# Routing of a mixture of experts rebuilt: top two with Max8 and an index search, running sums on TensorE, one-hots by two engines

## The chip, the cores and the metric

One core of a Trainium2 chip runs the whole program. Its five engines run side by side and meet at semaphores: TensorE (PE, matmul; its weight loads are listed as PEld), VectorE (DVE), ScalarE (ACT), GpSimd (POOL) and SyncE (SP), which here only issues transfers. The metric is the device time of one execution in microseconds, and of several executions their median.

## The reference

A decoder layer over 8 x 256 tokens of width 256: linear attention, a gated cross attention (mLSTM), and a mixture of 8 experts. The change touches only the routing in front of the experts:

```
normed = _layernorm(hidden_states, rn_g, rn_b)
logits = (jnp.einsum('bld,ed->ble', normed, router_w) + router_b).astype(jnp.float32)
top_w, top_idx = jax.lax.top_k(logits, K)                      # K = 2 of E = 8
top_w = jax.nn.softmax(top_w, axis=-1).astype(hidden_states.dtype)
onehot = jax.nn.one_hot(top_idx, E, dtype=top_w.dtype)
combine = jnp.einsum('blke,blk->ble', onehot, top_w)
for e in range(E):
    h = _layernorm(hidden_states, ln_g[e], ln_b[e])
    h = jax.nn.gelu(jnp.einsum('bld,di->bli', h, w1[e]) + b1[e], approximate=False)
    h = jnp.einsum('bli,id->bld', h, w2[e]) + b2[e]
    out = out + combine[..., e:e + 1] * h
```

## The kernel before

The 2048 tokens lie as T = 16 tiles of P = 128, token p of tile t in partition p. After the attentions, `mlstm_vector` normalizes the rows of batch b (two tiles) with `hidden_rows(b)`; ScalarE stores them to `hidden_rows` in memory with `store_rows(b)`, TensorE turns them and computes 8 logits per token in `logits(b)`, and `add_bias(b)` on VectorE moves the logits from PSUM to `LG` (T x E per partition). `logits(b)` waits for `add_bias(b - 2)`, since two PSUM banks serve in turn.

The experts work on slots, not on tokens. Every token has two pairs (token, expert), 4096 in all; the slots of an expert are filled in the order of tokens and padded to whole tiles of 128, which makes at most NT = 39 slot tiles. The routing must say for each slot tile which tokens stand in it (`tok_f`), with which weights (`wgt`), and whose expert it is (`tile_e`):

- `experts_vector` finds the greatest logit, its index, masks it out and does the same again (L1774 to L1783, each instruction over all 16 tiles and linked to the one ahead by a semaphore: `link`). `picked` is the sum of the two one-hot planes.
- TensorE counts along the partitions with two matmuls of `picked`: by a triangle (L1676, rank inside a tile) and by ones (L1677, count of each tile).
- VectorE scans these counts over the tiles, rounds the experts' totals up to whole tiles by counting thresholds, and adds up each pair's slot (L1794 to L1814). Three casts split the slot into slot tile and position in it (L1817 to L1820).
- For each of the 32 blocks of 128 pairs VectorE makes a 128-wide one-hot of the position (`posh`, L1825, eight blocks to an instruction) and three planes of 39 (L1830 to L1834: is it this slot tile, times token number, times weight). `posh` lies in `QT` where `hidden_rows` was staged, so the first waits for all stores (`z_st`).
- TensorE multiplies them, 32 accumulated matmuls of 3 x 39 columns (L1685): the result has, at partition p and column n, what slot p of slot tile n holds. Between the counts and these stand nine matmuls whose result nobody reads (`keep_going(9)`, L1673), and behind them six more.
- VectorE repairs the padding slots (L1849, L1850), casts the first token numbers (`tokg`) and signals `tok_r`. GpSimd then fetches the rows of slot tiles 0 and 1 from `hidden_rows` by an indirect transfer (L1640).

The tile loop follows: for each of 39 slot tiles TensorE turns the fetched rows (L1694), multiplies by the expert's `w1` (L1705), ScalarE applies Gelu (L1756), TensorE multiplies by `w2` (L1713), VectorE adds `b2` and scales (L1897, L1900), and GpSimd adds the rows to the output in memory (L1660). The output has been filled with X by SyncE before (L1627), as soon as all stores of `hidden_rows` have landed. The order on every engine is the order in which the code is written; there is no scheduler.

Of the kernel before, what the change touches and what calls it, by code (L numbers as in the profile page):

```python
# [29 lines left out]
C_TOK, C_CNT, C_TILE, C_RESET, C_PAR, C_CENT, C_PAD = 660, 692, 708, 748, 876, 878, 1006  # L30
C_POS, C_SLOT, C_W = 1007, 1135, 1174
# [34 lines left out]
def constants():  # L66
# [47 lines left out]
def build(nc, x_d, ctx_d, ctxr_d, idx_d, cst_d, wqT_d, wkT_d, wvT_d, woT_d, wk_d, gw_d, sw_d, wg_d, gb_d,  # L114
          rpe_d, lnw_d, lnb_d, rng_d, rnb_d, rw_d, rb_d, lg_d, lb_d, w1_d, b1_d, w2_d, b2_d, out_d):
    ctx = ExitStack()
    with ctx:
# [40 lines left out]
        first_slot = cst[:, C_SLOT:C_SLOT + NT]  # L158
# [886 lines left out]
        def parts_at(q):  # L1045
# [50 lines left out]
            sem("hid_r"), sem("hT_full"), sem("hT_cp"), sem("lg_full"), sem("lg_cp"), sem("z_st"))  # L1096
# [234 lines left out]
        def mlstm_scalar(act, at=None):  # L1331
# [103 lines left out]
            act.dma_start(z_dram[B * S:B * S + P], hid[0][:, 0]).then_inc(z_st, 16)  # L1435

        def mlstm_vector(dve):
# [122 lines left out]
            for b in range(4, B):  # L1560
                add_bias(b)
# [3 lines left out]
        def experts():  # L1565
            cl = Carve(PET[:, :, :].rearrange("p a b -> p (a b)"), kept)
            posh = QT[:, :, :, :].rearrange("p j b s -> p (j b s)").rearrange("p (k n) -> p k n", n=P)
            open_, base = cw(NT, E), cw(E)
            ntile, tile_end, tile_f, slot_f = cw(E), cw(E), cw(NT), cw(2 * T)
            b1c = [cw(I // P) for _ in range(2)]  # L1570
            fill_f, tok_f, wgt = cw(NT), cw(NT), cw(NT)
            LG2, EQ = cl(T, E), cl(T, E)
            OH = [cl(T, E) for _ in range(2)]
            picked, upto, slot_of = cl(E, T), cl(E, T), cl(E, T)
            over = LG2.rearrange("p t e -> p (t e)").rearrange("p (e t) -> p e t", e=E)
            M1, M2, IX, PR = cl(T), cl(T), cl(T), cl(T)
            pair_w, pos, first_of = cl(2 * T), cl(2 * T), cl(2 * T)
# [5 lines left out]
            f_ov, f_so, f_hit = sem("f_ov"), sem("f_so"), sem("f_hit")  # L1583
# [17 lines left out]
            NPOS = 8  # L1601
# [23 lines left out]
            def experts_sync(sp):  # L1625
                sp.wait_ge(z_st, 16 * (B + 1))
# [11 lines left out]
            def experts_gpsimd(pool):  # L1638
# [5 lines left out]
                pool.wait_ge(z_st, 16 * (B + 1))  # L1644
# [25 lines left out]
            def experts_tensor(pe):  # L1670
# [3 lines left out]

                pe.wait_ge(f_pk, 1)
                pe.matmul(bank(0, T * E), tri, picked.rearrange("p e t -> p (e t)"), start=True, stop=True)  # L1676
                pe.matmul(bank(1, T * E), ones, picked.rearrange("p e t -> p (e t)"), start=True, stop=True).then_inc(f_ps, 1)  # L1677

                keep_going(9)
                for k in range(2 * T):  # L1680
                    if k % T == 0:
                        pe.wait_ge(wts_r, k // T + 1)
                    if k % NPOS == 0:
                        pe.wait_ge(pos_r, k // NPOS + 1)
# [79 lines left out]
            def experts_vector(dve):  # L1764
# [4 lines left out]
                def wide(a):  # L1769
                    return a.unsqueeze(2).to_broadcast([P, T, E])  # L1770
# [373 lines left out]
```

## Time and profile before

| | us |
|---|---|
| median of three timed runs | 844.79 |
| lowest and highest of them | 840.76, 845.15 |
| the profiled execution, whole | 838.66 |
| its span | 836.9 |
| TensorE matmul busy in the span | 751.9 (90%) |
| VectorE busy | 403.1 (48%) |
| ScalarE busy | 353.4 (42%) |
| GpSimd busy | 429.7 (51%) |
| start of the first matmul of the tile loop | 544.22 |

The span is what the profile covers, and the whole time is that of the same execution with what lies around it. Positions below are microseconds from the span's start. A matmul of 32-bit numbers has two rows in the trace, so 32 of them are "x64". The granted clock of TensorE (PEclk) is a share of full speed.

### The profile page before, as it was taken

What the parts mean: (1) busy time and instruction counts of PE and PEld (TensorE: products, weight loads), DVE (VectorE), ACT (ScalarE), POOL (GpSimd) and SP (SyncE); (2) the same over time, 40 slices, a digit from 0 to 9 for tenths busy, and PEclk for the clock granted to TensorE, in tenths of its full rate; (3) what the DMA queues carried; (4) which work ended last, traced back from release to release, by engine and by line L of the source; (5) the groups of instructions that cost most, each with busy time, mean ns of one, the idle gap of its engine ahead of it and who ended that gap; (6) DMA issues with size and microseconds to landing.
All of it is one profiled execution on the core that took longest, in us unless ns stands there. A gap on an engine that the chain in (4) does not pass through costs nothing.

```text
span 836.9 us, 17067 instructions
## 1 busy us (share of the span) xinstructions
PE 751.9 (90%) x5866; PEld 662.0 (79%) x5867; DVE 403.1 (48%) x966; ACT 353.4 (42%) x916; POOL 429.7 (51%) x504
## 2 busy tenths in 40 slices
PE   7888888878988888898798887999999999999996
PEld 5566666657888878897787775689999999999995
DVE  2456666555554433332569897723333333333331
ACT  1333333324555433332667754144444444444441
POOL 6566666656666666666445541124444444444442
PEclk8999999989999999999889999999999999999999
DMA  9233333343233336356267699322221222122221
GB/s 293 78 102 103 109 113 111 111 121 93 84 92 89 89 89 189 89 108 194 83 185 202 201 282 354 120 77 38 38 38 32 37 38 38 31 38 38 38 36 22
DMA packets 75812, 88.29 MB, mean 106 GB/s; under 512 B 11952, under 2 KB 66032, under 8 KB 75632
## 3 DMA queue, kind: packets, MB, share of 16 engines
q0 software_dynamic: 19824, 43.93, 21.1%
q1 hardware_dynamic: 52256, 40.12, 16.5%
q10 hardware_dynamic: 3680, 3.54, 1.2%
q8 instruction: 34, 0.56, 0.3%
q14 instruction: 18, 0.15, 0.1%
HBM read 75.83 MB, written 11.73 MB: 105 GB/s over the span
## 4 chain that ended last, share of the span: by engine, by line
PE 40%; issue 27%; POOL 14%; DVE 9%; ACT 5%; another core or an unknown queue 3%; DMA 1%; POOLq 1%; DVEq 0%; ACTq 0%
PE ps L1964 15%; POOL out L1660 7%; PE ps L1030 7%; POOL G L1640 5%; PE ps L484 3%; PE ps L525 2%; PE ps L551 2%; DVE U L809 1%; ACT G L1353 1%; DMA out<-G,slots 1%; PE ps L1227 1%; PE ps L1673 1%; PE ps L592 1%; PE ps L477 1%
## 5 line engine op out<-in xcount | busy, mean ns | idle before, releaser
L331 POOL DMA_INDIRECT G<-in_rpe,hopi x193 | 186.6, 967 | 108.2 <-issue 42.1
L1756 ACT ACTIVATE G<-ps,U 128x128 f32<-128x128 f32 x312 | 84.9, 382 | 160.5 <-PE ps L1705 160.5
L1705 PEld LDWEIGHTS ps<-G,QT 128*128 128x128 f32 x1248 | 145.2, 192 | 1.9
L1705 PE MATMUL ps<-G,QT 128*128 128x128 f32 x1248 | 145.5, 275 | 0.0
L1713 PE MATMUL ps<-G 128*128 x624 | 141.2, 379 | 1.3 <-DVE G L1900 1.3
L1713 PEld LDWEIGHTS ps<-G 128*128 128x128 f32 x624 | 115.5, 190 | 15.8 <-issue 1.7
L1964 PE MATMUL ps<-U,PET 128*128 128x128 f32 (+3 forms) x768 | 104.2, 275 | 9.1 <-issue 8.7
L1964 PEld LDWEIGHTS ps<-U,PET 128*128 128x128 f32 x768 | 94.7, 192 | 14.6 <-issue 14.2
L978 DVE COPY PET<-ps 128x512 f32<-128x512 f32 x64 | 44.1, 690 | 116.1 <-PE ps L1030 99.3
L2007 ACT ACTIVATE PET<-ps 128x512 f32<-128x512 f32 (+1 forms) x63 | 37.4, 594 | 113.3 <-PE ps L1030 83.3
L1660 POOL DMA_INDIRECT out<-G,slots x39 | 66.7, 1711 | 24.4 <-issue 24.4
L1030 PE MATMUL ps<-cst,G 128*128 128x128 f32 x386 | 61.7, 276 | 7.0 <-issue 6.7
L1640 POOL DMA_INDIRECT G<-hidden_rows,slots x39 | 40.0, 1025 | 53.5 <-DVE U L1852 31.9
L676 ACT ACTIVATE U<-ps 128x512 f32<-128x512 f32 (+2 forms) x56 | 28.6, 512 | 72.9 <-remote 29.5
L809 DVE TENSOR_TENSOR U<-ps,cst 128x1024 f32<-128x1024 f32 x32 | 38.4, 1219 | 32.8 <-remote 14.2
L1870 DVE TENSOR_SCALAR G<-ps,U 128x128 f32<-128x128 f32 x78 | 28.4, 406 | 52.6 <-PE ps L1694 52.6
L1030 PEld LDWEIGHTS ps<-cst,G 128*128 128x128 f32 x386 | 46.4, 147 | 9.2 <-issue 8.7
L1665 POOL TENSOR_TENSOR U<-cst 128x1 f32<-128x1 f32 x39 | 7.4, 189 | 88.8 <-DMA out<-G,slots 88.8
L1741 ACT ACTIVATE QT<-U 128x1024 f32 x39 | 43.1, 1107 | 17.6 <-DVE U L1852 17.6
L331 POOL DMA_INDIRECT U<-in_rpe,hopi x38 | 37.1, 976 | 21.6 <-issue 10.4
L1257 PE MATMUL ps<-PET,G 128*128 128x99 f32 x256 | 41.9, 288 | 5.7 <-DVE G L1456 4.6
L1858 DVE TENSOR_SCALAR QT<-U 128x1024 f32 x39 | 27.1, 695 | 33.2 <-issue 33.2
(241 smaller groups left out, 1239.7 us busy)
## 6 DMA issues: line engine op xcount, KB each, us to landing
G<-run_max SPq DMA_DIRECT2D x16, 512.0 KB, 6.4
U<-in_w SPq DMA_DIRECT2D x16, 512.0 KB, 7.2
G<-in_w SPq DMA_DIRECT2D x8, 1024.0 KB, 10.2
G<-in_rpe,hopi POOLq DMA_INDIRECT x193
U<-in_ctx SPq DMA_DIRECT2D x8, 256.0 KB
tokens_kept<-X SPq DMA_DIRECT2D x8, 256.0 KB
X<-tokens_kept SPq DMA_DIRECT2D x1, 2048.0 KB
hidden_rows<-QT ACTq DMA_DIRECT2D x8, 256.0 KB, 7.4
```

The lines of the kernel that those rows point to most:

```text
L331: pool.indirect_dma_start(out=dst, out_offset=None, in_=rpe_d, in_offset=bass.IndirectOffsetOnAxis(ap=hopi[:, n:n + 1], axis=0)) \
L809: nc.vector.tensor_tensor(am[n % 2], s, tri.unsqueeze(1).unsqueeze(1).to_broadcast([P, 4, 2, P]), ALU.mult).then_inc(am_r, 1)
L978: copy(PET[:, q % NPT, 0:w], bank(turn_bank(q), 512)[:, 0:w]).then_inc(pet_r[q % 2], 1)
L1030: mm = pe.transpose(o[:, n % 2, j, :], src[:, j * P:(j + 1) * P], ident)
L1257: pe.matmul(o, Dm[u % ND][:, hh, c * P:(c + 1) * P], v[0], start=True, stop=(c == 0), skip_group_check=True)
L1640: pool.indirect_dma_start(out=z_in[u], out_offset=None, in_=z_dram, in_offset=bass.IndirectOffsetOnAxis(ap=tokg[:, u:u + 1], axis=0)) \
L1660: pool.indirect_dma_start(out=out_d, out_offset=bass.IndirectOffsetOnAxis(ap=tok[:, u:u + 1], axis=0), in_=ysb[u], in_offset=None, bounds_ ...
L1705: mm = pe.matmul(bank(1 + 2 * u + c // 4, 4, P)[:, c % 4], w1c[u][:, k, c], hT[u][:, k, :], start=(k == 0), stop=(k == KC - 1))
L1713: mm = pe.matmul(bank(7, 2, D)[:, u], gel[u][:, c, :], w2s[:, one(e), c, :].rearrange("p o n -> p (o n)"), start=(c == 0), stop=(c == NI - 1))
L1741: nc.scalar.activation(w1c[u][:, 1], w1_of(e, 1), ACT.Copy) \
L1756: ins = nc.scalar.activation(gel[u][:, c, :], bank(1 + 2 * u + c // 4, 4, P)[:, c % 4], ACT.Gelu, bias=b1c[u][:, c:c + 1])
L1964: mm = pe.matmul(o, pet[:, n % 2, j, :], rhs, start=True, stop=True, skip_group_check=True)
```

## The change

**Top two.** `mlstm_vector` no longer copies the last four batches' logits itself; it returns `add_bias`, and `experts_vector` calls it between pieces of the routing. `top_two(b0, b1)` issues a Max8 (`nc.vector.max`, the eight greatest of a row in order) for every tile of these batches, and then an index search (`max_index`) for every tile. Both work on 8 elements. The one-hot planes are compared from the indices, for tiles 0 to 13 ahead of the last batch, and for the last two behind it.

**Sums.** VectorE adds up `picked` over the tiles (`total`) and scans it (`ahead`). TensorE sums over partitions three times: `picked` by the triangle, `total` by ones, and `ahead` by ones, the last added onto the first in PSUM. The expert's padded start comes from adding 1.5 x 2^30, at which a 32-bit number keeps only multiples of 128; the slot tile is found in the same way, and the position by subtraction. The padding slots are preset by one matmul of a constant ahead of all (L1679), so that no repair is left behind the scatter matmuls.

**Fours.** One-hots and planes are made in eight chunks of four blocks. VectorE makes the planes of all and the one-hots of chunks 0, 1, 4 and 5; ScalarE makes the one-hots of 2, 3, 6 and 7 as relu(1 - |pos - p|), four Abs instructions and one Relu to a chunk. `z_st` is two semaphores: the first four chunks wait for the first four batches' stores, the others for all. The scatter matmuls take 2 x 39 columns, and `keep_going` is 3 and 4 long instead of 9 and 6.

```diff
@@ experts_tensor @@
+pe.matmul(bank(2, 2, NT), ident, cst[:, C_PAD:C_PAD + 2].unsqueeze(2).to_broadcast([P, 2, NT]), start=True, stop=False)
 pe.wait_ge(f_pk, 1)
-pe.matmul(bank(0, T * E), tri, picked.rearrange("p e t -> p (e t)"), start=True, stop=True)
-pe.matmul(bank(1, T * E), ones, picked.rearrange("p e t -> p (e t)"), start=True, stop=True).then_inc(f_ps, 1)
-keep_going(9)
+pe.matmul(bank(0, E, T), tri, picked[:, :, 1:T + 1], start=True, stop=False)
+pe.wait_ge(f_pk, 2)
+pe.matmul(bank(1, E), ones, total, start=True, stop=True).then_inc(f_ps, 1)
+pe.wait_ge(f_pk, 3)
+pe.matmul(bank(0, E, T), ones, ahead[:, :, 0:T], start=False, stop=True).then_inc(f_ps, 1)
+keep_going(3)
 for k in range(2 * T):
...
-    mm = pe.matmul(bank(2, NPL, NT), posh[:, k, :], load[:, :, k, :], start=(k == 0), stop=(k == 2 * T - 1))
+    mm = pe.matmul(bank(2, 2, NT), posh[:, c, k // 2 % 2, k % 2, :], load[:, 1:NPL, k, :],
+                   start=False, stop=(k == 2 * T - 1))
 mm.then_inc(filled_full, 1)
-keep_going(6)
+keep_going(4)
@@ experts_scalar @@
+act.wait_ge(z_st[0], 16 * (B // 2))
+act.wait_ge(pos_ok, 1)
+for h, c in enumerate(on_scalar):
+    if c == on_scalar[2]:
+        act.wait_ge(z_st[1], 16 * (B // 2 + 1))
+    for i in range(NPOS):
+        k = c * NPOS + i
+        ins = nc.scalar.activation(posh[:, c, i // 2, i % 2], in_tile_at, ACT.Abs, scale=-1.0, bias=pos[:, k:k + 1])
+    ins.then_inc(f_abs, 1)
+    act.wait_ge(f_abs, h + 1)
+    at = QT[:, :, c, :]
+    nc.scalar.activation(at, at, ACT.Relu, scale=-1.0, bias=ones[:, 0:1]).then_inc(pos_a, 1)
@@ experts_vector @@
+def top_two(b0, b1):
+    dve.wait_ge(lg_cp, b1)
+    for t in range(2 * b0, 2 * b1):
+        ins = nc.vector.max(top[:, t], LG[:, t])
+    link(ins)
+    for t in range(2 * b0, 2 * b1):
+        ins = nc.vector.max_index(at_e[:, t], top[:, t], LG[:, t])
+    return ins
...
+top_two(0, 2)
+add_bias(4)
+top_two(2, 4)
+add_bias(5)
+top_two(4, 6)
+add_bias(6)
+link(top_two(6, 7))
+link(one_hot_experts(0, T - 2))
+add_bias(7)
+pick(0, T - 2)
+link(top_two(7, 8))
+link(one_hot_experts(T - 2, T))
+pick(T - 2, T).then_inc(f_pk, 1)
+dve.wait_ge(f_pk, 1)
+nc.vector.tensor_reduce(out=total, in_=picked[:, :, 1:T + 1], op=ALU.add, axis=AX).then_inc(f_pk, 1)
...
+dve.wait_ge(f_ps, 1)
+link(nc.vector.tensor_scalar(rounded, bank(1, E), (P - 1) / 2, HIGH, ALU.add, ALU.add))
...
+nc.vector.scalar_tensor_tensor(pos, tile_h, HIGH, slot_1, ALU.subtract, ALU.subtract).then_inc(pos_ok, 1)
...
+for c in range(1, B):
+    open_tiles(c)
+    if c not in on_scalar:
+        if c == B // 2:
+            dve.wait_ge(z_st[1], 16 * (B // 2 + 1))
+        one_hot(c)
+    planes(c)
...
-link(nc.vector.tensor_scalar(fill_f, found[:, 0], 1.0, cst[:, C_PAD:C_PAD + 1], ALU.subtract, ALU.mult))
-link(nc.vector.tensor_tensor(tok_f, found[:, 1], fill_f, ALU.add))
-nc.vector.tensor_copy(tokg, tok_f[:, 0:2])
-nc.vector.tensor_copy(wgt, found[:, 2]).then_inc(tok_r, 1)
+nc.vector.tensor_copy(tokg, found[:, 0, 0:2]).then_inc(tok_r, 1)
+nc.vector.tensor_copy(tok_f, found[:, 0])
+link(nc.vector.tensor_copy(wgt, found[:, 1]))
```

On VectorE, from the last row of hidden states on, the order before is this (L1504 is `add_bias`, `x4` the last four batches; the names in brackets are the semaphores waited for):

```order
L1498 TENSOR_SCALAR QT<-X,U 128x256
L1504 TENSOR_TENSOR U<-ps,PET 128x16 [waits lg_full] x4
L1774 TENSOR_REDUCE PET<-U 128x16 [waits lg_cp]
L1775 TENSOR_TENSOR PET<-U,PET 128x128 [waits f_ch]
L1776 TENSOR_TENSOR PET<-PET,cst 128x128 [waits f_ch]
L1777 TENSOR_REDUCE PET<-PET 128x16 [waits f_ch]
L1778 TENSOR_TENSOR PET<-cst,PET 128x128 [waits f_ch]
L1780 TENSOR_SCALAR PET<-PET 128x128 [waits f_ch]
L1781 TENSOR_TENSOR PET<-PET,U 128x128 [waits f_ch]
```

In the changed kernel the same engine, from the seventh `add_bias` (now L1505) on, has this; four Max8 and four searches stand ahead of the fifth, of the sixth and of this seventh each:

```order
L1505 TENSOR_TENSOR U<-ps,PET 128x16 [waits lg_full]
L1796 MAX PET<-U 128x8 [waits lg_cp]
L1796 MAX PET<-U 128x8
L1799 MAX_INDEX PET<-PET,U 128x8 [waits f_ch]
L1799 MAX_INDEX PET<-PET,U 128x8
L1804 TENSOR_TENSOR PET<-cst,PET 128x2x112 [waits f_ch]
L1505 TENSOR_TENSOR U<-ps,PET 128x16 [waits lg_full,f_ch]
L1809 TENSOR_TENSOR PET<-PET 128x14x8
L1796 MAX PET<-U 128x8 [waits lg_cp]
L1796 MAX PET<-U 128x8
L1799 MAX_INDEX PET<-PET,U 128x8 [waits f_ch]
L1799 MAX_INDEX PET<-PET,U 128x8
```

The search for the top two has moved from behind the last logits to between them; two tiles of it remain behind the last `add_bias`.

On TensorE, behind the last logits (L1284), the order before is this (the semaphores' names in brackets are those under which they were first allocated: `sm_r` is `f_pk` here, `s_full` and `am_r` are `pos_r` and `wts_r`):

```order
L1284 MATMUL ps<-U,G 128x128 x3
L1676 MATMUL ps<-PET,cst 128x128 [waits sm_r]
L1677 MATMUL ps<-PET,cst 128x128
L1673 MATMUL ps<-X,cst 128x512 x9
L1685 MATMUL ps<-G,QT 128x117 [waits s_full,am_r]
L1685 MATMUL ps<-G,QT 128x117 x7
```

And in the changed kernel (`st_full` is `f_pk`, `s_full` is `wts_r`, `vp_r` the signal of VectorE's one-hots and `g_r` that of ScalarE's):

```order
L1285 MATMUL ps<-U,G 128x128 x3
L1679 MATMUL ps<-cst 128x78
L1681 MATMUL ps<-PET,cst 128x128 [waits st_full]
L1683 MATMUL ps<-PET,cst 128x8 [waits st_full]
L1685 MATMUL ps<-PET,cst 128x128 [waits st_full]
L1677 MATMUL ps<-X,cst 128x512 x3
L1696 MATMUL ps<-G,QT 128x78 [waits vp_r,s_full]
L1696 MATMUL ps<-G,QT 128x78 x3
L1696 MATMUL ps<-G,QT 128x78 [waits vp_r,s_full]
L1696 MATMUL ps<-G,QT 128x78 x3
L1696 MATMUL ps<-G,QT 128x78 [waits g_r,s_full]
L1696 MATMUL ps<-G,QT 128x78 x3
```

The scatter matmuls now wait at every fourth instead of every eighth, and a third count stands ahead of the fillers.

## Rows read from the trace of the kernel before

**Rows 1.** Chain of waits around the routing: start us, us, what.

```profile
515.61 1.86 PE ps L1284 x16
...
517.70 0.30 DVE PET L1774
...
521.95 0.49 PE ps L1676 x2
...
522.66 9.42 PE ps L1673 x18
532.08 7.15 PE ps L1685 x64
...
539.86 0.17 DVE slots L1851
...
540.89 1.05 POOL G L1640
```

**Rows 2.** Page, part 5, costliest groups: TensorE in the tile loop.

```profile
L1705 PE MATMUL ps<-G,QT 128*128 128x128 f32 x1248 | 145.5, 275 | 0.0
L1713 PE MATMUL ps<-G 128*128 x624 | 141.2, 379 | 1.3 <-DVE G L1900 1.3
```

**Rows 3.** Timeline of VectorE, 523 to 538: start us, us, instruction, idle before.

```profile
523.57 0.28 DVE L1799 TENSOR_TENSOR PET<-PET,ps 128x128 f32<-128x128 f32 x1
523.77 0.28 DVE L1801 TENSOR_REDUCE U<-PET 128x8 f32<-128x128 f32 x1
...
527.05 0.81 DVE L1830 TENSOR_TENSOR G<-cst,PET 128x624 f32<-128x624 f32 x1
527.89 0.81 DVE L1833 TENSOR_TENSOR G<-G,cst 128x624 f32<-128x624 f32 x1
528.62 0.80 DVE L1834 TENSOR_TENSOR G<-G,PET 128x624 f32<-128x624 f32 x1
...
533.89 2.35 DVE L1825 TENSOR_TENSOR QT<-cst,PET 128x1024 f32<-128x1024 f32 x2
536.16 0.48 DVE L1842 TENSOR_TENSOR U<-U,cst 128x312 f32<-128x312 f32 x1
...
537.18 0.18 DVE L1845 TENSOR_SCALAR tile_e<-U 128x39 int32<-128x39 f32 x1
```

**Rows 4.** Busy time in stretches: PE, PEld, DVE, ACT, POOL, PEclk, DMA share, GB/s.

```profile
413.00:414.00 1.00, 0.32 (x12) 0.13 (x4) 1.00 (x1) 1.00 (x4) 1.00 (x1) 0.66 0.62 198
...
523.00:524.00 1.00, 1.00 (x2) 0.33 (x1) 0.97 (x5) 0.47 (x1) 0.00 (x0) 0.50 0.29 102
...
531.00:532.00 1.00, 1.00 (x4) 0.46 (x3) 1.00 (x2) 0.00 (x0) 0.00 (x0) 1.00 0.95 314
```

**Rows 5.** Timeline of SyncE's queue: the copy of X to the output.

```profile
524.50 0.38 SPq L1627 DMA_DIRECT2D out<-X  x1
```

**Rows 6.** Timeline of VectorE, 509 to 523, columns as in rows 3.

```profile
509.01 0.26 DVE L1492 BATCH_NORM_AGGREGATE U<-U 128x2 f32<-128x6 f32 x2
...
513.88 0.17 DVE L1504 TENSOR_TENSOR U<-ps,PET 128x16 f32<-128x16 f32 x1 [0.38 <-PE ps L1284]
...
522.41 0.25 DVE L1789 RECIPROCAL PET<-PET 128x16 f32<-128x16 f32 x1
...
522.91 0.42 DVE L1794 TENSOR_TENSOR_SCAN PET<-cst,ps 128x128 f32<-128x128 f32 x1
```

**Rows 7.** Source line L1383, the eight stores of hidden rows: issue to landing.

```profile
DMA to landing us min/median/max: 6.1/7.4/8.9
```

**Rows 8.** Timeline of ScalarE, columns as in rows 3.

```profile
506.51 0.60 ACT L1395 ACTIVATE G<-ps 128x512 f32<-128x512 f32 x1 [0.17 <-PE ps L1273]
...
549.97 2.18 ACT L1756 ACTIVATE G<-ps,U 128x128 f32<-128x128 f32 x8 [6.88 <-PE ps L1705]
```

**Rows 9.** Timeline of TensorE in two stretches, columns as in rows 3.

```profile
412.38 0.71 PE L1239 MATMUL ps<-QT,G 32*128 32x256 f32 x8 [2.49 <-DVE G L1450]
...
539.05 5.33 PE L1673 MATMUL ps<-X,cst 128*128 128x512 f32 x12
```

More of the change, by code:

```diff
@@ L1559, in mlstm_vector @@
             hidden_rows(7)
-            for b in range(4, B):
-                add_bias(b)
+            return add_bias
         early.close()
@@ L1566, in experts @@
             cl = Carve(PET[:, :, :].rearrange("p a b -> p (a b)"), kept)
-            posh = QT[:, :, :, :].rearrange("p j b s -> p (j b s)").rearrange("p (k n) -> p k n", n=P)
-            open_, base = cw(NT, E), cw(E)
-            ntile, tile_end, tile_f, slot_f = cw(E), cw(E), cw(NT), cw(2 * T)
+            posh = QT[:, :, :, :].rearrange("p j b (i n) -> p b j i n", n=P)
+            open_, start, rounded, drop = cw(NT, E), cw(E + 1), cw(E), cw(E)
+            tile_f = cw(NT)
             b1c = [cw(I // P) for _ in range(2)]
[L1571 to L1577, printed above, removed]
+            tok_f, wgt = cw(NT), cw(NT)
+            slot_1, tile_h, pos, val = cw(2 * T), cw(2 * T), cw(2 * T), cw(2 * T)
+            top, at_e = cl(T, E), cl(T, E).bitcast(U32)
+            OH, hit = cl(2, T, E), cl(2, T, E)
+            picked, ahead = cl(E, T + 1), cl(E, T + 1)
+            slot_of = cl(E, T)
+            M2, PR, pair_w = cl(T), cl(T), cl(2 * T)
+            total = cl(E)
             pool_pad = cw(8)
@@ new lines, in experts_vector @@
+                dve.wait_ge(f_ps, 2)
+                link(nc.vector.tensor_tensor(slot_of, bank(0, E, T), start[:, 0:E].unsqueeze(2).to_broadcast([P, E, T]), ALU.add))
+                nc.vector.tensor_tensor(hit, OH, slot_of.rearrange("p e t -> p t e").unsqueeze(1).to_broadcast([P, 2, T, E]),
+                                        ALU.mult).then_inc(in_tile, 1)
+                dve.wait_ge(f_ex, 2)
+                nc.vector.reciprocal(pair_w[:, 0:T], PR).then_inc(f_ex, 1)
+                dve.wait_ge(in_tile, 2)
@@ new lines, in experts_vector, with of @@
+                link(nc.vector.tensor_reduce(out=slot_1.rearrange("p (k t) -> p k t", k=2), in_=hit, op=ALU.add, axis=AX))
+                nc.vector.tensor_scalar(tile_h, slot_1, -(P + 1) / 2, HIGH, ALU.add, ALU.add).then_inc(in_tile, 1)
+                dve.wait_ge(f_ex, 3)
+                nc.vector.tensor_tensor(pair_w[:, T:2 * T], M2, pair_w[:, 0:T], ALU.mult).then_inc(f_ex, 1)
+                dve.wait_ge(in_tile, 3)
+                def of(c):
+                    return slice(c * NPOS, (c + 1) * NPOS)
@@ new lines, in open_tiles, with planes @@
+                def open_tiles(c):
+                    nc.vector.tensor_tensor(load[:, 0, of(c)], first_high.unsqueeze(1).to_broadcast([P, NPOS, NT]),
+                                            tile_h[:, of(c)].unsqueeze(2).to_broadcast([P, NPOS, NT]), ALU.is_equal) \
+                        .then_inc(in_tile, 1)
+                def planes(c):
+                    dve.wait_ge(in_tile, 4 + c)
+                    for a, v in ((1, val), (2, pair_w)):
+                        ins = nc.vector.tensor_tensor(load[:, a, of(c)], load[:, 0, of(c)],
+                                                      v[:, of(c)].unsqueeze(2).to_broadcast([P, NPOS, NT]), ALU.mult)
+                    ins.then_inc(wts_r, 1)
```

153 lines of the change are left out of this document (63 added, 90 removed).

## The prediction

> **What bounds the kernel now.** I read four views in this order: the chain of waits, the three engines' timelines around the routing, the granted clock in stretches, and the two big groups of TensorE. The routing is the only work between the last router logits and the first fetch of rows for the experts. The chain of waits [rows 1] shows it as one serial path: TensorE ends the logits at 517.47, VectorE finds the top two experts in linked instructions from 517.70 until 521.9, TensorE counts (two matmuls) and then does its nine filler matmuls until 532.08, the 32 scatter matmuls of L1685 take 7.15 us, VectorE turns their result into token numbers, and GpSimd issues the first fetch at 540.89. That is 23.4 us from the last logit to the fetch. Behind it stand 39 tiles whose two TensorE groups, 145.5 and 141.2 us, fill nearly all of the rest with next to no idle time before them [rows 2]; nothing in that loop depends on how long the routing took, so a microsecond taken from the routing is a microsecond off the end.
>
> Three details decide what the change is worth. First, what the scatter matmuls wait for: VectorE has made their last one-hot at 533.89 + 2.35 = 536.24 [rows 3], yet they run without a pause from 532.08, because the fillers ended only then. Eight matmuls of 0.223 us (7.15/32) behind 536.24 would end at 538.0, so the fillers cost 1.2 us. Second, the clock: TensorE stood idle until 521.95, and at 523 its granted clock is 0.50, the lower level of 1.2 GHz; at 531 it is 1.00 again [rows 4]. Third, the data movers: they are busy until 532 [rows 4] with the copy of X into the output, issued at 524.50 [rows 5], as soon as the last rows of `hidden_rows` had landed.
>
> **VectorE's price list.** All its small instructions follow one law here. Not linked: a 128-element instruction starts 0.20 us after the one ahead, one of 624 elements takes 0.73 until the next start [rows 3], which is 0.06 us + 1.07 ns per element. Linked by a wait for its predecessor, the next start comes after 0.84 instead of 0.73 [rows 3], so a link costs 0.12 us.
>
> **Part 1, top two.** Removed: a chain of 13 linked instructions behind the last logit, 517.70 to 521.9 [rows 1]. Added: 16 Max8 and 16 index searches of 8 elements each. Most of them stand ahead of the last two `add_bias`, where VectorE is free: it falls idle at 513.50, 0.38 us ahead of the fifth batch's logits at 513.88 [rows 6], and then only waits for logits until 517.5. No row shows either instruction. The nearest are the small aggregates (two in 0.26, about 0.09 apart) from below and the reciprocal, which needs several cycles per element (0.25 for 16, 0.29 with a link), from above [rows 6]. I take 0.085 for Max8 and 0.15 for a search, nearer to the aggregates, since 8 elements in and 8 out are 16 steps of the law. The ends are 0.09 and 0.29 for both.
>
> The Trainium skill's page "Vector Engine (DVE) Microarchitecture Reference", section 3.9, describes the search as a load of the eight wanted values followed by FIND_INDEX_8. By that a search would be two passes, 0.15 to 0.17 by the law, and the sum would stay as it is; no row here shows it.
>
> Step by step: three memsets bring VectorE to 513.65. Four tiles cost 4 x 0.085 + 0.12 + 4 x 0.15 = 1.06. `add_bias(4)` is then at 514.8, `add_bias(5)` at 515.9 (TensorE wants it at 516.5 for the last logits, so nothing waits), `add_bias(6)` at 517.1. Two tiles with their links are 0.71 with a wait of 0.12 ahead (518.0), the wide one-hot 0.42 (518.4), the last bias and `pick` 0.28, two more tiles 0.71, the small one-hot and `pick` 0.42: `picked` is ready at 519.9 instead of 521.9. **Saves 2.0.**
>
> **Part 2, sums and slots.** The old way from 521.9 to the first plane at 527.05 [rows 1, 3] took 5.15 us in 20 instructions. Now: total (0.32), then the scan, which in the old kernel took 0.42 for 128 elements [rows 6], until 520.55; the third counting matmul, 0.49 by the old one [rows 1], until 521.05; then `slot_of` 0.32, `hit` of 256 elements 0.46, reduce 0.46, `tile_h` 0.22 and `pos`, at 522.6. That is 2.7 us for 5.15, **saves 2.4**. The exponent and the reciprocal lie in the gaps, where VectorE waits for links and TensorE.
>
> **Part 3, planes and one-hots in fours.** Old: 527.05 to 536.24, 9.2 us of VectorE. The three planes are still built whole; what leaves VectorE is half of the one-hots, which go to ScalarE. A chunk of four on VectorE is 0.23 + 0.61 + 0.46 = 1.30; one without the one-hot 0.23 + 0.12 + 0.46 = 0.81. From 522.7, with `val` 0.10: 4 x 1.30 + 4 x 0.81 = 8.4, planes ready at 531.3. **Saves 0.6 more**; against the old 536.24 the sum is 5.0. ScalarE's chunk is four Abs of 128 elements and one Relu of 512: eight 128-element activations with a pointer bias take 2.18 us, 0.27 each, and a 512-element one 0.60 [rows 8], so 3 x 0.27 + 0.38 + 0.68 with two links 1.9; four of them from 522.7 end at 530.3. That is 1 us ahead of VectorE, so it is hidden; were an Abs 0.38 without overlap, 2.3 a chunk, ScalarE would end at 531.9 and cost 0.5.
>
> Here a rule speaks against the change. The rows price a one-hot chunk at 0.61 on VectorE and 1.9 on ScalarE, so the work as such gets three times dearer and only the split pays: with all eight chunks on VectorE the planes end 4 x 0.49 = 2.0 later. The Trainium skill's page "ScalarE: Activation LUTs", section "Rules for kernel authors", says to use VectorE, not ScalarE, for relu and its like. By that rule nothing would move and the gain would be 5.5 instead of 7.5.
>
> The waits on the stores: a store lands within 8.9 us [rows 7]. The first four batches are issued ahead of 513.5, where VectorE has the eighth ready [rows 6], so they are in by 522.4, before VectorE or ScalarE ask. The last four have landed by 524.5 [rows 5]; VectorE asks for them at about 526.7. The first is covered narrowly by this bound, the second by 2 us.
>
> **Part 4, TensorE.** Three fillers instead of nine: 0.89 us each at full clock (12 rows, two to a matmul, in 5.33 [rows 9]), twice that at the lower, so from 521.05 they end between 523.7 and 525.5 and set nothing: even from 525.5 the matmuls catch up with the chunks (0.9 us of matmul against 1.05 of VectorE) and are at most 0.4 late. Making them 78 columns wide instead of 117 I cost at nothing: 117 columns come 0.223 apart, and eight matmuls of 128 columns took 1.86, 0.23 apart [rows 1], so the columns do not set the pace; were they to, the last chunk would be 0.3 shorter. The last chunk, ready at 531.3, ends at 532.2. Old: 539.23. **Gain 7.0.**
>
> **Part 5, to the fetch.** Old: two linked instructions and a cast from 539.23 to 540.03 [rows 1], and a copy of 0.09 before the signal. New: `tile_e` is ready 1.2 us behind the planes (536.16 to 537.36 [rows 3]), at 532.5, then one cast of 0.17: 532.65 against 540.12. **Gain 7.5 in all.** The fetch goes out at 533.4, still behind the copy of X (data movers at 0.95 at 531 [rows 4]); a routing 1.5 us faster yet would run into it. Four fillers instead of six now end at about 535.8, so TensorE idles some 1 us ahead of the first turn.
>
> **The sum.** 838.66 - 7.5 = 831.2 for the profiled execution, whose span is 836.9. The median of the three timed runs is 844.79, 6.1 above the profiled one, and I subtract from it: **837.3 us**, 0.9% less. 0.5% is 4.2 us, about what a measurement of this kernel can tell from no change (the three runs lie between 840.76 and 845.15).
>
> **Rivals.**
> 1. The clock falls again. TensorE idles 2.4 us ahead of `picked` (517.5 to 519.9). An idle stretch of 2.49 us at 412.38 [rows 9] was followed by 0.66 [rows 4], so such a gap can be enough. If it falls at 521, the fillers hide it. If it falls around the wait for the first rows, the first tile's matmuls run at half rate for 3 us, which costs 1.5: gain 6, 838.8. With both and a late ScalarE 5: 839.8. For it: fewer fillers (7 for 15). Against it: the scatter matmuls fill 0.85 of the stretch before.
> 2. Max8 and search are dear. At 0.29 each four tiles take 2.44, `add_bias(5)` comes at 518.6 and holds up the last logits, and `picked` is ready at 525.3: 5.4 later than above, gain 2.1, 842.7, no measurable change. **The other side:** the same mechanism at 0.36 an instruction (32 of them, one microsecond per 0.03) takes back all, and above 0.49 the kernel is slower by over 0.5%: 849. Against it: neither of the 8- and 16-element neighbours [rows 6] is over 0.26.
> 3. Both are cheap, 0.09: `picked` is bound by the last logit and ready at 519.0. The gain is 8.4, 836.4.
> 4. The gain is real at the fetch and given back in the loop, because a transfer of the first tiles (the table `b2`, the copy of X) is then late: 841 to 843. For it: the copy of X ends at 532, close to where the new fetch begins. Against it: two TensorE groups without idle time before them [rows 2].
>
> **How the numbers follow.** My forecast with rival 3: 0.63. Rival 1: 0.17. Rival 2 at its upper row: 0.08, and slower by it: 0.04. Rival 4: 0.08. Faster by over 0.5% (below 840.6) is the first two, 0.80; within, 0.16; slower, 0.04. The range holds 8 of 10: downward the cheap search and a median that falls where the lower runs of before lie (three to four microseconds), 832.5; upward rival 1 and part of 2 and 4, 841.5.
>
> **What would show it.** In the profile of the changed kernel: Max8 0.08 to 0.09 apart and a search 0.15; the counting matmuls starting at 519.9; `pos` at 522.6; the last plane at 531.3 with ScalarE's last Relu about 1 us ahead of it; the scatter matmuls in eight bursts, the last ending at 532.2; the first fetch issued at 533.4; the granted clock at 1.00 from 526 to the second tile. The forecast is wrong if the distance from the last logit to the fetch is not 16 us, or if what stands behind the fetch is longer than the 296 us of before.

## The result and the profile after

The changed kernel takes 837.54 us (median of 8 runs, 833.74 to 840.12) where the kernel before takes 844.97 (8 runs, 840.76 to 848.28): a ratio of 0.9924 with an interval of 0.9900 to 0.9949, so between 4.3 and 8.4 us less. The forecast was 837.3.

The profiled execution took 837.07 us, against 838.66 before, with a span of 835.2. It reached the end of the last logits at 521.72, the old one at 517.46. These 4.26 us lie ahead of the routing. In that stretch the mean granted clock was 0.95 where the old one had 0.97; that this made the difference is likely and not shown. So I measure everything from the last logit. Two distances then tell the whole: from the last logit to the issue of the first fetch, and from there to the end of the span.

| us | last logit to fetch | fetch to end |
|---|---|---|
| before | 23.4 | 296.0 |
| after | 15.9 | 297.6 |

The chain of waits of the changed kernel, which answers [rows 1]: start us, us, what.

```profile
523.59 0.49 PE ps L1681 x2
...
533.64 2.92 PE ps L1696 x24
536.65 0.17 DVE slots L1897
...
537.61 1.30 POOL G L1643
```

The counting starts at 523.59, 1.9 behind the last logit instead of 4.5; the last burst of scatter matmuls (L1696, two rows to a matmul) stands directly ahead of the cast, with no fillers between VectorE's last plane and it; and the fetch goes out at 537.61.

VectorE's timeline of the changed kernel, which answers [rows 3] and [rows 6]: start us, us, instruction, idle before.

```profile
518.76 0.36 DVE L1796 MAX8 PET<-U 128x8 f32<-128x8 f32 x4
...
519.31 0.07 DVE L1799 MATCH_VALUE_LOAD PET<-PET,U 128x8 f32 x1
519.37 0.16 DVE L1799 FIND_INDEX8 PET<-PET,U 128x8 uint32<-128x8 f32 x1
519.45 0.07 DVE L1799 MATCH_VALUE_LOAD PET<-PET,U 128x8 f32 x1
...
525.18 0.60 DVE L1842 TENSOR_TENSOR PET<-PET 128x256 f32<-128x256 f32 x1
...
526.48 0.19 DVE L1873 SCALAR_TENSOR_TENSOR U<-U 128x32 f32<-128x32 f32 x1
...
527.99 0.31 DVE L1857 TENSOR_TENSOR G<-cst,U 128x156 f32<-128x156 f32 x1
...
529.28 0.31 DVE L1857 TENSOR_TENSOR G<-cst,U 128x156 f32<-128x156 f32 x1
...
534.91 0.31 DVE L1864 TENSOR_TENSOR G<-G,PET 128x156 f32<-128x156 f32 x1
```

Four Max8 take 0.36, and a search is two rows, MATCH_VALUE_LOAD and FIND_INDEX8, one pair every 0.14 (519.31 to 519.45). `pos` is there at 526.67 (526.48 + 0.19). A chunk with its one-hot on VectorE goes from 527.99 to 529.28, 1.29. The last plane of the last chunk ends at 535.22.

ScalarE's timeline, which answers [rows 8]: the one-hots of chunks 6 and 7.

```profile
530.63 1.26 ACT L1756 ACTIVATE QT<-cst,U 128x128 f32<-128x128 f32 x4
...
532.55 1.26 ACT L1756 ACTIVATE QT<-cst,U 128x128 f32<-128x128 f32 x4
533.85 0.72 ACT L1760 ACTIVATE QT<-QT,cst 128x512 f32<-128x512 f32 x1
```

Four Abs and a Relu take 1.92 (530.63 to 532.55), and the last Relu ends at 534.57, 0.65 ahead of VectorE.

TensorE's timeline, which answers [rows 9], and the granted clock, which answers [rows 4] (PE, PEld, DVE, ACT, POOL busy, then PEclk, DMA share, GB/s).

```profile
519.71 2.01 PE L1285 MATMUL ps<-U,G 128*128 128x128 f32 x16
...
524.58 2.74 PE L1677 MATMUL ps<-X,cst 128*128 128x512 f32 x6
528.12 1.12 PE L1696 MATMUL ps<-G,QT 128*128 128x78 f32 x8 [0.80 <-DVE G L1864]
...
536.38 3.64 PE L1677 MATMUL ps<-X,cst 128*128 128x512 f32 x8
540.79 0.44 PE L1706 MATMUL ps<-cst,G 128*128 128x128 f32 x2 [0.76 <-DMA G<-hidden_rows,slots]
...
542.66 9.00 PE L1717 MATMUL ps<-G,QT 128*128 128x128 f32 x64
```

```profile
543.00:544.00 1.00, 1.00 (x7) 1.00 (x7) 0.79 (x3) 0.00 (x0) 0.00 (x0) 0.58 0.42 98
544.00:545.00 1.00, 1.00 (x7) 1.00 (x6) 0.00 (x0) 0.00 (x0) 0.86 (x1) 0.50 0.82 270
547.00:548.00 1.00, 1.00 (x11) 1.00 (x10) 0.00 (x0) 0.00 (x0) 0.00 (x0) 1.00 0.15 61
```

The first two groups of w1 matmuls (L1717, x64) take 9.00 us. In the kernel before the same 64 rows took 7.37:

```profile
546.03 7.37 PE L1705 MATMUL ps<-G,QT 128*128 128x128 f32 x64
```

The clock shows why: it was 0.58 and 0.50 in the first microseconds of the tile loop, and 1.00 again at 547. That is 1.63 us, which is what stands between 297.6 and 296.0.

### The profile page after: what moved, and what is told of

It is laid out like the page before. It is cut to its first block, busy times and chain, and to the rows that moved or that the text cites. A ratio compares the mean times of both kernels' runs of the same rounds, so it can differ in the third digit from the quotient of the medians.

```text
span 835.2 us, 17124 instructions
## 1 busy us (share of the span) xinstructions
PE 752.2 (90%) x5854; PEld 669.5 (80%) x5855; DVE 404.5 (48%) x1018; ACT 361.6 (43%) x936; POOL 433.1 (52%) x504
## 4 chain that ended last, share of the span: by engine, by line
PE 40%; issue 27%; POOL 15%; DVE 10%; ACT 5%; another core or an unknown queue 2%; DMA 1%; POOLq 1%; DVEq 0%; ACTq 0%
PE ps L2011 15%; POOL out L1664 8%; PE ps L1031 7%; POOL G L1643 5%; PE ps L485 3%; PE ps L552 2%; PE ps L526 2%; PE ps L478 2%; ACT G L1354 2%; DMA out<-G,slots 1%; DVE U L810 1%; PE ps L450 1%; ACT G L1355 1%; PE ps L1228 1%
## 5 line engine op out<-in xcount | busy, mean ns | idle before, releaser
L1717 PEld LDWEIGHTS ps<-G,QT 128*128 128x128 f32 x1248 | 146.9, 194 | 2.0
L1717 PE MATMUL ps<-G,QT 128*128 128x128 f32 x1248 | 147.2, 277 | 0.0
L2011 PE MATMUL ps<-U,PET 128*128 128x128 f32 (+3 forms) x768 | 106.3, 281 | 9.7 <-issue 9.5
L2011 PEld LDWEIGHTS ps<-U,PET 128*128 128x128 f32 x768 | 98.7, 198 | 12.1 <-issue 11.7
L1664 POOL DMA_INDIRECT out<-G,slots x39 | 69.3, 1776 | 23.6 <-issue 23.6
L1031 PE MATMUL ps<-cst,G 128*128 128x128 f32 x386 | 63.8, 283 | 6.7 <-issue 6.6
L810 DVE TENSOR_TENSOR U<-ps,cst 128x1024 f32<-128x1024 f32 x32 | 38.4, 1220 | 36.4 <-PE ps L552 17.7
L1031 PEld LDWEIGHTS ps<-cst,G 128*128 128x128 f32 x386 | 48.3, 152 | 8.5 <-issue 8.3
```

What stands on the lines that cost most here:

```text
L810: nc.vector.tensor_tensor(am[n % 2], s, tri.unsqueeze(1).unsqueeze(1).to_broadcast([P, 4, 2, P]), ALU.mult).then_inc(am_r, 1)
L1031: mm = pe.transpose(o[:, n % 2, j, :], src[:, j * P:(j + 1) * P], ident)
L1664: pool.indirect_dma_start(out=out_d, out_offset=bass.IndirectOffsetOnAxis(ap=tok[:, u:u + 1], axis=0), in_=ysb[u], in_offset=None, bounds_ ...
L1717: mm = pe.matmul(bank(1 + 2 * u + c // 4, 4, P)[:, c % 4], w1c[u][:, k, c], hT[u][:, k, :], start=(k == 0), stop=(k == KC - 1))
L2011: mm = pe.matmul(o, pet[:, n % 2, j, :], rhs, start=True, stop=True, skip_group_check=True)
```

## The experiments

They ran on three chips, on which the kernel before takes 784 us (medians 784.44, 784.41 and 783.98) instead of 845. Most of these 60 us lie ahead of the routing: the last logit ends at 461 to 464 instead of 517. For each experiment I give both distances, beside 15.9 and 297.6 of the changed kernel (23.4 and 296.0 of the kernel before). Each kernel has one profiled execution here, so a distance is that of a single execution; where no median is given, the kernel ran only once. Where program and clock are the same, positions agree within 0.1 us: the counts start 1.85 to 1.87 behind the last logit in every kernel with the top two as changed.

**Top two behind the logits.**

```diff
-top_two(0, 2)
-add_bias(4)
-top_two(2, 4)
...
-link(top_two(7, 8))
-link(one_hot_experts(T - 2, T))
-pick(T - 2, T).then_inc(f_pk, 1)
+for b in range(4, B):
+    add_bias(b)
+link(top_two(0, 8))
+link(one_hot_experts(0, T))
+pick(0, T).then_inc(f_pk, 1)
```

> The changed kernel with all Max8 and index searches behind the last logits, none between them. Theory A: what was gained at this part comes from the place, not from the instructions; 16 Max8 at 0.075 and 16 searches at 0.145 with their links and the one-hots take 4.6 to 4.8 us, as long as the old chain of 13 (4.5), so counting starts 2.9 us later and the distance from last logit to fetch is 18.8, up to 19.3 if the clock falls in the longer gap. Rival: the instructions themselves are the gain and the distance is 16.5 or less.

Measured: 19.6, 0.3 above the most that theory A had, and 297.6; median 780.29 (10 runs), ratio to the kernel before 0.9944 (0.9923 to 0.9966). VectorE's timeline: 16 Max8, the last search, and `pick`; and TensorE's behind it.

```profile
461.56 1.19 DVE L1796 MAX8 PET<-U 128x8 f32<-128x8 f32 x16
...
464.89 0.16 DVE L1799 FIND_INDEX8 PET<-PET,U 128x8 uint32<-128x8 f32 x1
...
465.55 0.37 DVE L1809 TENSOR_TENSOR PET<-PET 128x128 f32<-128x128 f32 x1
```

```profile
467.42 5.31 PE L1677 MATMUL ps<-X,cst 128*128 128x512 f32 x6
472.54 7.30 PE L1696 MATMUL ps<-G,QT 128*128 128x78 f32 x64
```

From 461.56 to 465.92 (465.55 + 0.37) is 4.36 us, about as long as the old chain of 13 linked instructions, 4.2 [rows 1]. So at this size Max8 and the search gain nothing by themselves; their place between the logits brings 2.8 (the counts start 4.7 behind the last logit instead of 1.9). The other 0.9 of the 3.7 that this kernel loses goes with the clock, which fell at the counts: the three fillers took 5.31 instead of 2.74, and the scatter matmuls ran behind them without a pause and ended 0.9 later behind the counts. The 3.7 are a loss in the distance of one execution. The medians do not show them: this kernel gains 4.2 us on the kernel before, as much as the changed kernel did when it ran again (see "The changed kernel again"). The two ran on different chips and were not compared directly, and what the clock takes from execution to execution is as large as this part.

**All one-hots on VectorE.**

```diff
-on_scalar = (2, 3, 6, 7)
+on_scalar = ()
```

> The changed kernel with the one-hots of all eight chunks on VectorE and none on ScalarE. Theory A: VectorE sets the pace with 1.30 us a chunk instead of 0.82 where ScalarE helped, so from the last logit to the fetch it takes 15.9 + 4 x 0.48 = 17.8. Rival (the rule that such work belongs on VectorE): two engines at work slow each other, VectorE's instructions get shorter alone and the distance stays at 15.9 to 16.3.

Measured: 17.7 and 296.6, as theory A had it. TensorE's bursts, each started by VectorE's planes:

```profile
469.89 1.12 PE L1696 MATMUL ps<-G,QT 128*128 128x78 f32 x8 [0.18 <-DVE G L1864]
471.19 1.12 PE L1696 MATMUL ps<-G,QT 128*128 128x78 f32 x8 [0.18 <-DVE G L1864]
```

The eight bursts come 1.30 apart, which is what a chunk with its one-hot took on VectorE in the changed kernel, where ScalarE worked beside it (1.29): VectorE was not slowed by that. The split is worth 1.8 us.

**One wait for all stores.**

```diff
 dve.wait_ge(z_st[0], 16 * (B // 2))
+dve.wait_ge(z_st[1], 16 * (B // 2 + 1))
 one_hot(0)
```

The same line was added ahead of ScalarE's first Abs.

> The changed kernel with the first one-hots of VectorE and ScalarE waiting for all stores of the hidden rows, as before, not for the first half. Theory A: the last store lands 6.6 us behind the last logit and the first one-hot starts 5.2 behind it, so the first one-hot starts 1.3 us later and the distance from last logit to fetch is 17.2 instead of 15.9. Rival: the wait is covered, as one wait for the first half was: 15.9.

Measured: 17.7 and 297.8; theory A had 17.2. The first one-hot on VectorE:

```profile
469.71 0.69 DVE L1870 TENSOR_TENSOR QT<-cst,U 128x512 f32<-128x512 f32 x1 [1.53 <-DMA hidden_rows<-QT]
```

It starts 7.0 behind the last logit instead of 5.2. The wait is 1.53; the other 0.28 lies ahead, at the third count, which ran at the lower clock. So the split of the wait was needed to keep 1.5 us of the faster routing; my prediction counted the stores as covered and gave this no price.

**The fillers ahead.** Three kernels: the one before with three instead of nine, the changed one with nine, and with none.

```diff
-keep_going(9)
+keep_going(3)
```

> The kernel before with three filler matmuls instead of nine between counts and scatter. Theory A: the fillers end later than VectorE and cost 1.2 us, so from the last logit to the fetch it takes 22.2 instead of 23.4. Rival: the fillers buy the clock; without six of them TensorE idles from about 527 to 530.5 after a stretch at 0.50, stays at or falls back to 0.50, and the scatter matmuls take longer than they gain: 23.4 or more.

Measured: 25.4 and 296.2, so 2.0 more to the fetch than the kernel before. TensorE, then its clock:

```profile
467.15 4.50 PE L1673 MATMUL ps<-X,cst 128*128 128x512 f32 x6
475.25 10.08 PE L1685 MATMUL ps<-G,QT 128*128 128x117 f32 x64 [3.60 <-DVE QT L1825]
```

```profile
476.00:477.00 1.00, 1.00 (x6) 1.00 (x6) 0.96 (x3) 0.00 (x0) 0.00 (x0) 0.50 0.00 0
480.00:481.00 1.00, 1.00 (x7) 1.00 (x6) 1.00 (x2) 0.00 (x0) 0.00 (x0) 0.53 0.00 0
481.00:482.00 1.00, 1.00 (x11) 1.00 (x11) 0.84 (x3) 0.00 (x0) 0.00 (x0) 1.00 0.00 0
```

The fillers end at 471.65, TensorE idles 3.60 us, and the 32 scatter matmuls take 10.08 us instead of 7.15 [rows 1]: the clock fell in that gap, was at 0.50 until 480 and at 1.00 from 481 on. The rival was right, in this one execution. The old nine fillers were not 1.2 us of waste: they paid for the clock of the matmuls behind them. Whether seven or eight would have done was not tried.

```diff
-keep_going(3)
+keep_going(9)
```

> The changed kernel with nine fillers ahead of the scatter matmuls, as before. Theory A: they end 8.0 us after their start at 2.9 behind the last logit, and 7.15 us of scatter matmuls follow without a pause, so the distance from last logit to fetch is 15.9 + 3.4 = 19.3: the shorter fillers were needed to cash in the rest. Rival: VectorE's planes are the bound and it stays 15.9.

Measured: 18.9 and 296.1; theory A had 19.3.

```profile
465.56 7.89 PE L1677 MATMUL ps<-X,cst 128*128 128x512 f32 x18
473.29 7.27 PE L1696 MATMUL ps<-G,QT 128*128 128x78 f32 x64
```

The scatter matmuls follow without a pause. So in the changed kernel nine would have eaten 3.0 of the 7.5 us.

```diff
-keep_going(3)
+keep_going(0)
```

> The changed kernel without the three filler matmuls between counts and scatter. Theory A: TensorE is idle for about 3.2 us, its clock falls to 0.50 for some 3 us while scatter matmuls run at 0.46 us each, and they end about 1.2 us later: 17.1 from last logit to fetch. Rival: the fillers are idle weight, the clock stays and the distance is 15.9.

Measured: 21.7 and 296.2, 4.6 above theory A and 5.8 above the rival. TensorE, and its clock early and late in the matmuls:

```profile
470.36 13.94 PE L1696 MATMUL ps<-G,QT 128*128 128x78 f32 x64 [3.37 <-DVE G L1864]
```

```profile
470.00:471.00 1.00, 0.64 (x3) 0.64 (x4) 1.00 (x4) 0.97 (x3) 0.00 (x0) 0.50 0.48 170
...
483.00:484.00 1.00, 1.00 (x7) 1.00 (x7) 0.00 (x0) 0.00 (x0) 0.00 (x0) 0.50 0.00 0
```

That the clock falls in the gap was expected. That it stays at the lower level through 13.9 us of matmuls without a pause was not: 0.43 us a matmul instead of 0.223, to the last of them.

**Six fillers behind.**

```diff
 mm.then_inc(filled_full, 1)
-keep_going(4)
+keep_going(6)
```

> The changed kernel with six filler matmuls behind the scatter matmuls, as before, instead of four. The changed kernel takes 15.9 us from the last logit to the first fetch (before: 23.4) and 297.6 us from there to the end (before: 296.0); at the first tile's w1 matmuls its granted clock is 0.50 to 0.58 for 3 us, and the two first groups of 32 take 9.00 us instead of 7.37. Theory A: the fall comes from the gap that two fillers fewer leave ahead of the first tile. Then the clock stays 1.00, the two groups take 7.4, the distance from fetch to end is 296.0, and the whole gains 1.6 on the changed kernel (some 9 us on the kernel before). Rival: the fall comes from the 1.2 us gap between the two first turns, which stays; then 9.0 and 297.6 again. Second rival: the fillers hold up the first turn; then the fetch to end distance is 0.3 to 1 longer than 296.0.

Measured: 19.9 and 298.7 in the profiled execution, which was the slowest of ten (783.51; the fastest 776.46). The median is 778.25, its ratio to the kernel before 0.9927 (0.9901 to 0.9953). The edit lies behind the scatter matmuls, and the loss ahead of it. TensorE, then its clock:

```profile
465.92 2.74 PE L1677 MATMUL ps<-X,cst 128*128 128x512 f32 x6
469.46 1.12 PE L1696 MATMUL ps<-G,QT 128*128 128x78 f32 x8 [0.80 <-DVE G L1864]
470.75 11.14 PE L1696 MATMUL ps<-G,QT 128*128 128x78 f32 x56 [0.18 <-DVE G L1864]
481.69 7.32 PE L1677 MATMUL ps<-X,cst 128*128 128x512 f32 x12
```

```profile
471.00:472.00 1.00, 1.00 (x11) 1.00 (x11) 0.96 (x4) 0.97 (x4) 0.00 (x0) 0.99 1.02 352
472.00:473.00 1.00, 1.00 (x7) 1.00 (x6) 1.00 (x4) 1.00 (x5) 0.00 (x0) 0.50 1.03 346
...
481.00:482.00 1.00, 1.00 (x6) 1.00 (x6) 0.00 (x0) 0.00 (x0) 0.00 (x0) 0.50 0.00 0
```

Up to 471 everything is as in the changed kernel, to 0.03 us. Then the clock falls, in the middle of the scatter matmuls, and as in the kernel without fillers ahead it does not come back while they last. There 4.0 us are lost (19.9 for 15.9). The six fillers, begun at the lower level, took 7.32 and held up the first turn: this is the second rival in kind, but at 2.7 (298.7 for 296.0), where it had at most 1. None of the three theories named the fall among the scatter matmuls. At the first tile the clock was 1.00 and the 64 rows took 7.37, as theory A had it.

**Wide scatter matmuls.** The kernel with six fillers and the changed one are the same program up to the last scatter matmul, and the clock fell in different places. That left two questions: is the place chance, and why did the clock stay down? In both profiles in which it stayed down to the last scatter matmul these had 78 columns. In the kernel before with three fillers, where it was down as they began, they had 117, and it came back during them. That kernel differs in more than the columns.

```diff
-pe.matmul(bank(2, 2, NT), ident, cst[:, C_PAD:C_PAD + 2]...
+pe.matmul(bank(2, NPL, NT), ident, cst[:, C_PAD - 1:C_PAD + 2]...
...
-    mm = pe.matmul(bank(2, 2, NT), posh[...], load[:, 1:NPL, k, :],
+    mm = pe.matmul(bank(2, NPL, NT), posh[...], load[:, :, k, :],
```

First without fillers, where the clock fell with 78 columns, as the pair to that kernel.

> 117 columns in the scatter matmuls and no fillers ahead of them; beside it stands the run with 78 columns and no fillers, where the clock fell behind the counts, stayed at 0.50 through all 13.9 us of scatter matmuls and came back only in the fillers behind them (21.7 from last logit to fetch). Theory A: the clock falls in the same gap, and comes back during the wide matmuls within 3 to 6 us: 17.3 to 18.5. Rival: it stays down to the end again, 21.7.

Measured: 17.1 and 296.3.

```profile
467.53 9.68 PE L1696 MATMUL ps<-G,QT 128*128 128x117 f32 x64 [3.37 <-DVE G L1864]
```

```profile
467.00:468.00 1.00, 0.47 (x2) 0.47 (x3) 1.00 (x5) 0.97 (x3) 0.00 (x0) 0.50 0.82 289
...
473.00:474.00 1.00, 1.00 (x11) 1.00 (x11) 0.96 (x4) 0.95 (x3) 0.00 (x0) 1.00 1.03 349
```

The clock fell to 0.50 in the same gap and was 1.00 again at 473, 5.5 us into the matmuls, which ended 9.7 us after their start instead of 13.9. That is theory A, 0.2 below its range. The programs of this pair differ in nothing but the columns, but there is one execution of each. With the kernel of six fillers and the kernel before with three, that is two of two that stayed down with 78 and two of two that came back with 117. The clock did not fall at the same moment in these four, so chance is not ruled out, and why is open.

> The changed kernel with all three planes in the scatter matmuls again, 117 columns instead of 78. Theory A (the narrow matmuls are what lets the clock stay at the lower level): the pace stays at 0.223 us a matmul, so with the clock up the distance from last logit to fetch is 15.9, and if it falls it is back within about 6 us, in the scatter matmuls: at most 18. Its median is then 0 to 2 us below the changed kernel's on this chip. Rival (columns do not matter, the fall is chance alone): as likely as for the changed kernel to show 19 to 20.

Measured: 15.9 and 297.7; median 776.58 (6 runs), ratio 0.9910 (0.9880 to 0.9939). The distance is that of the narrow matmuls, so with the clock up the columns cost nothing, as the prediction had it. Among the scatter matmuls the clock did not fall here, so this execution says nothing on theory A. At the first tile it fell as in the first profile of the changed kernel.

**The changed kernel again.**

> The changed kernel once more, unchanged. Five kernels that share its program up to the scatter matmuls or its fillers showed the clock fall to 0.50 in different places: at the first tile, in the middle of the scatter matmuls (where it stayed down to their end, 3.7 us lost), or at the counts. Theory A: where it falls differs from execution to execution of one program; this look shows another place than the first look at the same kernel (fetch 15.9 behind the last logit, then 297.6), with 15.9 to 20 and 296 to 298.7. Rival: the place belongs to the program, and it shows 15.9 and 297.6 again.

Measured: 16.1 and 296.0; median 779.81 (10 runs, 776.42 to 782.26), ratio 0.9944 (0.9922 to 0.9965). TensorE:

```profile
467.31 4.22 PE L1677 MATMUL ps<-X,cst 128*128 128x512 f32 x6
471.37 4.86 PE L1696 MATMUL ps<-G,QT 128*128 128x78 f32 x40
476.40 2.90 PE L1696 MATMUL ps<-G,QT 128*128 128x78 f32 x24 [0.18 <-DVE G L1864]
...
485.40 7.37 PE L1717 MATMUL ps<-G,QT 128*128 128x128 f32 x64
```

Another place than in the first profile: the clock fell at the counts, so the three fillers took 4.22 instead of 2.74, and came back in them; the scatter matmuls caught up, 0.25 us late. The first tile ran at 7.37. So the place differs from execution to execution of one program. On this chip the changed kernel gains 4.2 us (2.7 to 6.1), not 7.4; the intervals of the two comparisons overlap.

**Put together.** Two versions. One is the changed kernel with six fillers behind and the two product planes as one instruction; the other adds the wide matmuls and a fourth filler ahead.

```diff
-for a, v in ((1, val), (2, pair_w)):
-    ins = nc.vector.tensor_tensor(load[:, a, of(c)], load[:, 0, of(c)],
-                                  v[:, of(c)].unsqueeze(2).to_broadcast([P, NPOS, NT]), ALU.mult)
+ins = nc.vector.tensor_tensor(load[:, 1:3, of(c)], load[:, 0:1, of(c)].to_broadcast([P, 2, NPOS, NT]),
+                              both[:, :, of(c)].unsqueeze(3).to_broadcast([P, 2, NPOS, NT]), ALU.mult)
```

> The changed kernel with six fillers behind the scatter matmuls and the two product planes of a chunk as one VectorE instruction of 312 elements instead of two of 156. Theory A: one start of 0.06 us less per chunk, 0.5 us for eight, ScalarE then being about as late as VectorE: 15.4 from last logit to fetch; and 296.0 from there to the end if the fillers hold the clock. Together 2.1 us less than the changed kernel and 9.5 less than the kernel before. Rival: the four-dimensional access or ScalarE's one-hots set the pace and the distance stays 15.7 to 15.9; if the clock falls all the same, 297.6 behind it.

Measured: 15.8 and 296.7; median 776.93 (4 runs), ratio 0.9897 (0.9881 to 0.9914), so 7.5 us below the kernel before and not 9.5. The planes ended 0.3 sooner by the last logit, though the third count was 0.37 late; the clock had fallen at the counts, so TensorE, not VectorE, ended last.

> The changed kernel with 117 columns, the two product planes as one instruction, four fillers ahead of the scatter matmuls and six behind. Theory A: 15.3 to 15.8 from last logit to fetch, 296 to 296.7 behind it, and a median 9 to 10 us below the kernel before, 2 below the changed kernel in the same comparison. Rival: falls of the clock at the counts are left and take it to 16 to 17, no better than the changed kernel.

Measured: 15.5 and 296.8; median 777.31 (6 runs), ratio 0.9907 (0.9882 to 0.9931). The distances are those of theory A, but the median is 6.7 us below the kernel before, and not 9 to 10. The clock stayed at 1.00 from the last logit through the first tiles. TensorE behind the scatter matmuls:

```profile
476.82 5.32 PE L1678 MATMUL ps<-X,cst 128*128 128x512 f32 x12
481.98 0.38 PE L1707 MATMUL ps<-cst,G 128*128 128x128 f32 x2
```

The sixth filler ends at 482.14, and the first transposes start 4.9 behind the cast instead of 4.1, so it takes back 0.8. With the clock up, five might do; that was not tried. In the same comparison the changed kernel had 779.81, the wide one 776.58 and this one 777.31; both are 2.5 to 3.2 us below it, but the intervals of the ratios overlap, so that they beat it is likely and not shown.

## Why the prediction was right, step by step

- **The path.** Right: the routing alone moved, and it moved the end. From the last logit to the fetch it took 15.9; the text said 16.
- **Part 1, saves 2.0.** It saved 2.6 (1.9 behind the last logit against 4.5). Every piece was a little cheaper than its price: a search took 0.14 for 0.15, as two instructions, a Max8 0.07 for 0.085 (16 in 1.19), and four tiles with their link 0.96 (518.76 to 519.72) for 1.06; the memsets, priced at 0.15, did not show. That most of the work moves between the logits was in the step, and the kernel with everything behind the logits showed that this place brings the gain.
- **Part 2, saves 2.4.** 523.59 to 526.67 is 3.1 us for my 2.7: from `hit`, a product of broadcasts over 256 elements, it was 0.67 to the next linked instruction for 0.46 (525.18 to 525.85), `slot_of` started 0.1 behind the third count, and `pos` takes 0.19 itself. So 2.1.
- **Part 3, 5.0 in all.** 1.29 and 0.82 a chunk against 1.30 and 0.81, ScalarE 1.92 against 1.9, its end 0.65 ahead of VectorE against 1. Right; from the last logit to VectorE's last plane or one-hot it was 13.5 instead of 18.8, so 5.3 in all. The rule of the Trainium skill ("ScalarE: Activation LUTs", "Rules for kernel authors") that relu belongs on VectorE would have cost 1.8 here, measured, for the 2.0 that I gave it.
- **The stores.** Right that they are covered, but counted as nothing: a single wait as before costs 1.5. It is the split of the semaphore that covers them.
- **Part 4, gain 7.0.** Right in the sum: the scatter matmuls end 14.8 behind the last logit, 21.8 before, so 7.0. Errors cancelled on the way: the last plane came 0.3 sooner than forecast, and the last matmul 1.3 behind it for 0.9. Wrong in one figure: three fillers at twice 0.89 from 521.05 end at 526.4 and not at 525.5, and the matmuls are then 1.3 late, not "at most 0.4 late". The kernel with the top two behind the logits ran so: its fillers took 5.31, and the matmuls behind them were 0.9 late. In doubt is "Making them 78 columns wide instead of 117 I cost at nothing". It costs nothing while the clock is up. In the execution in which it fell among them, that of six fillers behind, it stayed down to their end, which cost 4.0; that the columns were the cause is not shown.
- **Rival 1.** It had 0.17, and in 4 of the 9 profiles with four fillers behind, the clock fell at the first tile, for some 1.6 us each (I had said 1.5); with six, in none of 5. In the profiled execution it took 1.6 of the 7.5, so that execution gained 5.9 behind the last logit, as rival 1 has it. By my own sign the forecast failed in that execution: what stands behind the fetch is longer than the 296 us of before. The median of eight gained 7.4. That it came out at the forecast's own number is partly luck: the clock took 1.6 us in one profiled execution of the changed kernel, 0.2 in the other, and 6.7 in that of six fillers, and in the other comparison 4.2 was left.
- **Rivals 2 to 4.** Max8 and search were not dear. Rival 3 came in part: the counts started 1.9 behind the last logit, where the forecast had 2.4 and the rival 1.5. The copy of X collided with nothing (fetch to end is 296.0 to 296.8 in all profiles but the four with the fall at the first tile and the one in which six fillers began at the lower level).
- **The range** of 832.5 to 841.5 holds the median and all eight runs.

## What to carry to other kernels

A serial stretch between two busy ones is worth timing from its own start, step by step, with a price for an unlinked and a linked instruction: the sum here came out within 0.1 us of 16, though its steps were off by up to 0.6 both ways. Instructions that find something for small tiles gained here by being issued as the tiles arrive, not by being fewer. And a matmul whose result nobody reads may be paying for the clock of those behind it: take such fillers away only where the granted clock of several executions shows that it stays.

## What the runs showed of the hardware that I had not expected

- The granted clock fell at different places in different executions of one program: in the changed kernel once at the first tile and once at the counts, and in the kernel of six fillers, the same program up to there, among the scatter matmuls. One profile of a kernel cannot tell which is usual.
- Back-to-back 32-bit matmuls of 78 columns, weights changed each time, ran at 0.50 for 13.9 and for some 9.9 us and the clock did not come back before their end, at 0.43 us each; in the two profiles with 117 columns it came back 5.5 and 5.7 us into them. At the upper level 32 of them took 7.27 and 7.15 us, so the columns do not show in the pace there.
- The Trainium skill's page "TensorE: Matmul & The Clock Gate", section "What's actually happening", says that activity releases the throttle. The traces agree where the clock came back, as in the fillers of the changed kernel's second profile; in the two executions with 78 columns it stayed at 0.50 to the end of 13.9 and some 9.9 us of matmuls without a pause.
- Max8 over 8 elements takes 0.07 us from start to start (16 in 1.19), a MATCH_VALUE_LOAD with its FIND_INDEX8 0.14.
